# Keys through DRAM, one rounded maximum, and the low halves on VectorE in a fused attention and feed-forward block

## Chip, cores and metric

One NeuronCore of a Trainium2 chip runs the whole block in one launch. The metric is the device time in microseconds. Before the change the median of three runs is 3265.69 us (3263.84 to 3275.1).

## The reference

For 64 batches of 256 positions with 512 channels, and a context of the same shape:

```python
q, k, v = relu(heads(layernorm(x))), relu(heads(ctx)), relu(heads(ctx))   # 16 heads of 32
att = softmax(q @ k.T / sqrt(32))
x = x + tanh(g_xattn) * relu(concat(att @ v) @ ffn_w.T + ffn_b)
xn = layernorm(x); prev = xn shifted by one position (zero first)
r = sigmoid((mu_r * xn + (1 - mu_r) * prev) @ W_r.T)
k2 = (mu_k * xn + (1 - mu_k) * prev) @ W_k.T
x = x + tanh(g_ffn) * r * (square(relu(k2)) @ W_v.T)
```

## The kernel before

Products that need more than one rounded pass are made of two rounded halves, a high one (the value rounded to fp32r) and a low one (what the rounding left): high times high, low times high, high times low. Each tensor that enters such a product is thus split by two instructions: a rounding copy on ScalarE (`..._high`) and a difference (`..._low`). For the scores the three terms are stacked along the contraction: `q_st` and `k_st` hold, for each head, 96 rows of 32 channels (three combinations of halves), in four groups c of four heads.

The loop is software-pipelined by hand over the batches: `pipeline` (L203) runs `iteration(i, par)` on each engine, and each engine has its own written order. In one turn i, TensorE does the sixteen `shifted_scores(i, n)` with `scores` seven ahead (up to `scores(i + 1, 6)`), `values` and `denominators` of each group once the group's exponentials are there, and between them, in 32 pieces, the dense products of earlier batches: `key` (i - 2), `project` (i - 1), `receptance` and `value` (i - 2). Two banks of PSUM alternate for the scores, so `scores(n)` waits until `head_max(n - 2)` has read its bank; two more alternate for the shifted scores. One bank, `tp_bank`, serves all transposes (`turn_q`, `turn_m`, `turn_xn`) in turn. Engines wait only on semaphores; what stands behind a wait in an engine's order waits too.

Around the change, by engine:

- SyncE (L217): `load_k` (L242) loads the keys of group c three times, once for each 32-row block of `k_raw`; `load_x`; `move_m` (L251) moves the two halves of the negated maxima into rows 96 and 97 of `q_st`; `write_o` and `read_o` turn the attention's output through DRAM; `store`.
- GpSimd (L312): `rstd_1`, `rstd_2` (a power on one or two columns), and the low halves `k_low` (L335), `o_low` (L350), `xk_low`, `xr_low`, `ka_low`, the difference `x_diff` (L358) of neighbouring positions and the square `ka_square` (L384).
- ScalarE (L430): `k_high` (L480) writes relu(k), rounded, to all 96 rows of `k_st` and relu(k) in place in 32 rows of `k_raw`; the exponentials (L489); `q_stack` (L471) and `xt_copy` copy transposes out of `tp_bank`; `load_x1` and `load_v` issue transfers; other high halves.
- VectorE (L638): `head_max` (L688) reduces a bank of scores to `nmax`; `split_m` (L698) splits four heads' maxima into two halves, which `turn_m` then transposes and `copy_m` (L708) copies out; `norm_o` (L715) is a reciprocal of the denominators and a product, and waits for `denominators`; `add_x`, `norm_2`, `mix_k` (L750), `mix_r`, `stats_1` (L652), `finish` (L770), `relu_v` (L683), `q_low` (L675).
- TensorE (L857): `project(b, u)` (L965) starts with the bias product, then waits for `o_hi_ready` and `o_lo_ready`; `values` waits for `v_ready`.

VectorE's order in a turn begins with head_max 7 of batch i and ends with head_max 6 of batch i + 1; the other work stands between maxima, as in `head_max(i, 12)`, `copy_m(i, 2)`, `q_low(i + 1, 1)`, `norm_o(i, 0)`, `head_max(i, 13)`. TensorE's order there is `shifted_scores(i, 5)`, dense, `scores(i, 12)`, dense, `values(i, 0)`, `turn_m(i, 2)`, `denominators(i, 0)`, `shifted_scores(i, 6)`, `turn_q`, then the first piece of `project(i - 1, 1)`.

## Time and profile before

| | before |
|---|---|
| median of three runs | 3265.69 us |
| the profiled execution's own time | 3260.97 us |
| its span, first to last instruction | 3259.0 us |
| granted TensorE clock, mean | 0.987 |
| TensorE busy | 2905.3 us (89%) |
| VectorE busy | 2953.6 us (91%) |
| ScalarE busy | 2040.9 us (63%) |
| GpSimd busy | 1669.2 us (51%) |
| DMA | 308.95 MB, 95 GB/s, mean busy share of the 16 engines 31% |

A busy share is an average over the span. Which engine ends last at a given place is read in the timeline, from the idle time before an instruction and what released it. A matmul's end is modelled, so TensorE's busy time isn't its rate at its peak.

### The profile page before, as it was taken

To read this page: it belongs to the slowest core of one execution; us is meant where nothing else is said; L and a number is where in the kernel's file an instruction comes from. 1 tells how busy PE (TensorE), PEld (TensorE's weight loads), DVE (VectorE), ACT (ScalarE), POOL (GpSimd) and SP (SyncE) were. 2 spreads that over 40 slices of the span, in tenths; PEclk is the share of its full clock that TensorE was granted. 3 is DMA by queue.
4 is the path that set the end of the run, shared out by engine and by line. 5 is a ranking of instruction groups with operands and counts; after the bars stand their busy time and mean duration, and the time that the engine had idled before them with its cause. 6 is when DMAs were issued, how large, how long until landed. Compare 5 with 4: busy or idle time off the path is not lost. (4 is left out here: it accounts for less than half of the span.)

```text
span 3259.0 us, 74168 instructions
## 1 busy us (share of the span) xinstructions
PE 2905.3 (89%) x23168; PEld 2204.9 (68%) x23168; DVE 2953.6 (91%) x4559; ACT 2040.9 (63%) x3276; POOL 1669.2 (51%) x1158
## 2 busy tenths in 40 slices
PE   3899899999999999999899999999999999999998
PEld 2567666666667667667676666666666676666776
DVE  4899999999999999999999999999999999999984
ACT  4566666666666666666666666666666666666662
POOL 1455555555554554555555555545545545545553
PEclk9899999999999999999999999999999999999999
DMA  3333323323323323333233233233233233232331
GB/s 106 95 89 104 102 83 105 104 81 103 105 84 102 101 87 97 93 98 101 82 106 102 83 105 104 81 105 106 81 103 103 85 102 100 87 99 88 100 94 38
DMA packets 289548, 308.95 MB, mean 95 GB/s; under 512 B 162529, under 2 KB 197345, under 8 KB 289506
## 3 DMA queue, kind: packets, MB, share of 16 engines
q1 hardware_dynamic: 254690, 241.30, 25.0%
q10 hardware_dynamic: 34816, 67.12, 6.1%
q8 instruction: 24, 0.39, 0.0%
q14 instruction: 18, 0.15, 0.0%
HBM read 239.08 MB, written 67.11 MB: 94 GB/s over the span
## 5 line engine op out<-in xcount | busy, mean ns | idle before, releaser
L346 POOL TENSOR_TENSOR k_st<-k_raw,k_st 32x1024 fp32r<-32x1024 f32 x256 | 617.6, 2412 | 774.8 <-ACT k_raw L487 761.4
L694 DVE TENSOR_REDUCE nmax<-bank 128x2 f32<-128x512 f32 x1024 | 683.7, 684 | 64.3 <-PE bank L916 55.3
L498 ACT ACTIVATE probs<-bank 128x512 f32<-128x512 f32 x1024 | 595.2, 592 | 234.0 <-PE bank L928 229.7
L916 PE MATMUL bank<-k_st,q_st 96*128 96x256 f32 x2048 | 442.2, 298 | 79.1 <-DVE nmax L694 74.0
L916 PEld LDWEIGHTS bank<-k_st,q_st 96*128 96x128 f32 x2048 | 357.1, 193 | 160.4 <-DVE nmax L694 95.4
L723 DVE RECIPROCAL o_val<-bank 128x256 f32<-128x256 f32 x256 | 447.2, 1747 | 13.8 <-PE bank L954 9.9
L484 ACT ACTIVATE k_st<-k_raw 96x1024 fp32r<-96x1024 f32 x256 | 270.6, 1057 | 295.6 <-DMA k_raw<-ctx_t_dram 295.5
L928 PE MATMUL bank<-q_st,k_st 98*128 98x256 f32 x2048 | 441.4, 297 | 13.6 <-DMA q_st<-m_t 10.8
L928 PEld LDWEIGHTS bank<-q_st,k_st 98*128 98x128 f32 x2048 | 348.2, 192 | 85.4 <-issue 26.7
L476 ACT ACTIVATE q_st<-bank 96x512 fp32r<-96x512 f32 x512 | 303.0, 592 | 158.7 <-PE bank L884 157.1
L961 PE MATMUL bank<-xk_hi,w_hi 128*128 128x256 f32 x1024 | 299.0, 292 | 0.0
L942 PE MATMUL bank<-probs,v_pos 128*32 128x256 f32 x4096 | 278.1, 389 | 13.0 <-DVE v_pos L686 7.3
L961 PE MATMUL bank<-xk_lo,w_hi 128*128 128x256 f32 x1024 | 286.9, 280 | 0.0
L961 PE MATMUL bank<-xk_hi,w_lo 128*128 128x256 f32 x1024 | 286.8, 280 | 0.0
L954 PE MATMUL bank<-probs,ones_r 128*32 128x256 f32 x4096 | 280.7, 393 | 0.0
L487 ACT ACTIVATE k_raw<-k_raw 32x1024 f32<-32x1024 f32 x256 | 270.4, 1056 | 8.1
L884 PE MATMUL bank<-ident_r,q_nat 128*96 128x128 f32 x2048 | 220.7, 231 | 48.8 <-ACT q_st L476 31.3
L884 PEld LDWEIGHTS bank<-ident_r,q_nat 128*96 128x96 f32 x2048 | 191.4, 127 | 103.7 <-issue 73.5
L355 POOL TENSOR_TENSOR o_lo<-o_mv,o_hi 128x512 fp32r<-128x512 f32 x128 | 166.4, 1300 | 178.4 <-ACT o_hi L505 166.7
L388 POOL TENSOR_TENSOR xm<-xm 128x512 f32<-128x512 f32 x128 | 141.7, 1107 | 183.4 <-ACT xm L542 175.8
L757 DVE SCALAR_TENSOR_TENSOR xm<-xd,mu_sb,xt 128x256 f32<-128x256 f32 x256 | 229.9, 956 | 5.1 <-POOL xd L364 5.1
L332 POOL TENSOR_TENSOR rstd<-ve,mhalf 128x1 f32<-128x1 f32 x128 | 69.2, 541 | 300.0 <-DVE ve L741 185.6
(93 smaller groups left out, 7055.8 us busy)
## 6 DMA issues: line engine op xcount, KB each, us to landing
k_raw<-ctx_t_dram SPq DMA_DIRECT2D x768, 128.0 KB, 2.5
x_ln<-x_dram SPq DMA_DIRECT2D x256, 128.0 KB
v_pos<-ctx_dram ACTq DMA_DIRECT2D x64, 512.0 KB, 5.5
o_dram<-o_val SPq DMA_DIRECT2D x256, 128.0 KB, 1.7
o_mv<-o_dram SPq DMA_DIRECT2D x512, 64.0 KB, 2.1
x<-x_dram ACTq DMA_DIRECT2D x64, 512.0 KB, 3.3
out_dram<-x SPq DMA_DIRECT2D x64, 512.0 KB, 2.9
q_st<-m_t SPq DMA_DIRECT2D x512, 4.0 KB
```

The source lines that it names most:

```text
L346: nc.gpsimd.tensor_tensor(k_st[rows, c, :, :], k_raw[rows, :, :], k_st[rows, c, :, :].bitcast(F32), ALU.subtract).then_inc(k_lo_ready, 1)
L476: nc.scalar.activation(q_st[0:QK, c, :, P * u:P * u + P], tp_bank[0:QK, :].rearrange("p (g t) -> p g t", g=GR), ACT.Copy).then_inc(q_stack ...
L484: nc.scalar.activation(k_st[0:QK, c, :, :], k_raw[0:QK, :, :], ACT.Relu).then_inc(k_hi_ready, 1)
L498: nc.scalar.activation(probs[:, n // GR % 2, n % GR, :, :].rearrange("p v t -> p (v t)"), st_bank[n % 2][:, :], ACT.Exp, scale=SCALE).then ...
L694: nc.vector.tensor_reduce(nmax[:, :, n % GR:n % GR + 1], s_bank[n % 2][:, :].rearrange("p (u y) -> p u y", u=NU), AX_X, ALU.max, negate=Tr ...
L723: nc.vector.reciprocal(o_val[:, :], pv_bank[:, T:2 * T]).then_inc(rden_ready, 1)
L884: mm = nc.tensor.transpose(tp_bank[0:QK, P * g:P * g + P].bitcast(F32R), q_nat[:, u, GR * c + g, :, :], ident_r[:, :])
L916: mm = nc.tensor.matmul(s_bank[n % 2][:, T * u:T * u + T], q_st[0:QK, c, g, P * u:P * u + P], k_st[0:QK, c, g, :], start=True, stop=True)
L928: mm = nc.tensor.matmul(st_bank[n % 2][:, T * v:T * v + T], k_st[0:ST, c, g, P * v:P * v + P], q_st[0:ST, c, g, :], start=True, stop=True)
L942: nc.tensor.matmul(pv_bank[HD * g:HD * g + HD, 0:T], v_pos[:, v, HD * h:HD * h + HD], probs[:, c % 2, g, v, :], start=(v == 0), stop=(v == ...
L954: mm = nc.tensor.matmul(pv_bank[HD * g:HD * g + HD, T:2 * T], ones_r[:, 0:HD].bitcast(F32), moving, start=(n == 0), stop=(n == len(sums) - 1))
L961: mm = nc.tensor.matmul(dst, lhs[a], rhs[c], start=first and n == 0, stop=last and n == 2)
```

## The change

1. Keys. Each batch's keys are loaded once, 128 partitions by four groups (`load_k(b)`, four transfers). ScalarE rounds them in one instruction into a new tile `k_high` (`k_halve`), VectorE leaves the low half in `k_raw` (`k_low(b)`), both halves are written to a tensor `k_dram` in DRAM (`write_k`), and `stack_k` reads them back into the 96 rows of `k_st`, two transfers for each group. This begins two batches ahead, so the pipeline starts one iteration earlier. `k_high` of four groups on ScalarE and `k_low` of four groups on GpSimd go.
2. Maxima. They are written rounded by `head_max` itself, `split_m` goes, one row of `q_st` in place of two holds them, and `move_m` is one transfer.
3. `o_low`, `x_diff`, `xk_low`, `xr_low` and `ka_low` go from GpSimd to VectorE, `ka_square` to ScalarE. GpSimd keeps `rstd_1` and `rstd_2`.

```diff
@@ sync
-            def load_k(b, c):
-                    after(sp, k_hi_ready, CH * b + c)
-                    after(sp, k_lo_ready, CH * b + c)
-                    for r in range(3):
-                        sp.dma_start(k_raw[HD * r:HD * r + HD, :, :],
-                                     ctx_t[b][:, GR * c:GR * c + GR, :]).then_inc(k_loaded, 16)
+            def load_k(b):
+                    for g in range(GR):
+                        sp.dma_start(k_raw[g:P:GR, :, :],
+                                     ctx_t[b].rearrange("f (c g) t -> g f c t", g=GR)[g]).then_inc(k_loaded, 16)
+            def write_k(b, par):
+                    sp.wait_ge(k_hi_ready, b + 1)
+                    sp.wait_ge(k_lo_ready, b + 1)
+                    for half, tile in enumerate((k_high, k_raw)):
+                        sp.dma_start(k_dram[par, :, half].rearrange("c f g t -> (f g) c t"),
+                                     tile[:, :, :]).then_inc(k_written, 16)
+            def keys_written(b):
+                    sp.wait_ge(k_written, 32 * (b + 1))
+            def stack_k(b, c, par):
+                    after(sp, st_ready, HEADS * (b - 1) + GR * c + GR)
+                    sp.dma_start(k_st[0:2 * HD, c, :, :].bitcast(F32),
+                                 k_dram[par, c].rearrange("h f g t -> (h f) g t")).then_inc(k_stacked[c], 16)
+                    sp.dma_start(k_st[2 * HD:QK, c, :, :].bitcast(F32), k_dram[par, c, 0]).then_inc(k_stacked[c], 16)
             def iteration(i, par):
-                load_k(i, 3)
+                stack_k(i, 3, par)
                 store(i - 3, 1 - par)
                 move_m(i, 1)
                 write_o(i - 1, 3)
                 read_o(i - 1, 1)
-                load_k(i + 1, 0)
+                keys_written(i + 1)
+                load_k(i + 2)
+                stack_k(i + 1, 0, 1 - par)
                 move_m(i, 2)
                 write_o(i, 0)
-                load_k(i + 1, 1)
+                stack_k(i + 1, 1, 1 - par)
                 load_x(i + 2)
                 move_m(i, 3)
                 write_o(i, 1)
-                load_k(i + 1, 2)
+                stack_k(i + 1, 2, 1 - par)
                 move_m(i + 1, 0)
                 load_w(i)
                 read_o(i, 0)
                 write_o(i, 2)
+                write_k(i + 2, par)
@@ scalar
+            def k_halve(b):
+                    act.wait_ge(k_loaded, 16 * GR * (b + 1))
+                    after(act, k_written, 32 * b)
+                    nc.scalar.activation(k_high[:, :, :].bitcast(F32R), k_raw[:, :, :], ACT.Relu).then_inc(k_hi_ready, 1)
+            def ka_square(b, half):
+                    nc.scalar.activation(part, part, ACT.Square).then_inc(ka_ready, 1)
...
@@ vector
+            def k_low(b):
+                    dve.wait_ge(k_hi_ready, b + 1)
+                    nc.vector.scalar_tensor_tensor(out=k_raw[:, :, :].bitcast(F32R), in0=k_raw[:, :, :], scalar=0.0,
+                                                   in1=k_high[:, :, :], op0=ALU.max,
+                                                   op1=ALU.subtract).then_inc(k_lo_ready, 1)
             def iteration(i, par):
                 head_max(i, 7)
-                split_m(i, 1)
...
                 copy_m(i, 2)
                 q_low(i + 1, 1)
                 norm_o(i, 0)
+                o_low(i - 1, 1)
                 head_max(i, 13)
+                xr_low(i - 2)
...
                 norm_o(i, 1)
+                ka_low(i - 2, 0)
                 head_max(i + 1, 1)
+                ka_low(i - 2, 1)
+                x_diff(i - 1, 0)
                 head_max(i + 1, 2)
+                x_diff(i - 1, 1)
                 mix_k(i - 1)
                 head_max(i + 1, 3)
-                split_m(i + 1, 0)
                 copy_m(i + 1, 0)
                 head_max(i + 1, 4)
                 stats_1(i + 2)
                 finish(i - 2, 0, par)
+                xk_low(i - 1, 0)
                 head_max(i + 1, 5)
                 norm_o(i, 2)
+                xk_low(i - 1, 1)
                 head_max(i + 1, 6)
+                k_low(i + 2)
+                o_low(i, 0)
```

On ScalarE `ka_square` stands right behind each `kt_relu`, and `k_halve(i + 2)` behind `xt_copy(i - 1, 1)`. On TensorE `turn_m` waits for `head_max`'s own count, and `scores` of a group's first head wait for `k_stacked[c]`.

## Rows read from the trace of the kernel before

**Rows 1.** The page's first part: busy time of each engine.

```profile
span 3259.0 us, 74168 instructions
PE 2905.3 (89%) x23168; PEld 2204.9 (68%) x23168; DVE 2953.6 (91%) x4559; ACT 2040.9 (63%) x3276; POOL 1669.2 (51%) x1158
```

**Rows 2.** Timeline, TensorE: start, duration (us), engine, line, tiles, shape, count, idle before.

```profile
1506.45 1.07 PE L954 MATMUL bank<-probs,ones_r 128*32 128x256 f32 x16
...
1516.60 0.28 PE L893 MATMUL bank<-ident_r,m_nat 128*8 128x128 f32 x2 [1.11 <-DVE m_nat L705]
...
1527.58 0.28 PE L893 MATMUL bank<-ident_r,m_nat 128*8 128x128 f32 x2 [0.70 <-DVE m_nat L705]
...
1540.38 1.07 PE L942 MATMUL bank<-probs,v_pos 128*32 128x256 f32 x16
...
1541.59 1.07 PE L954 MATMUL bank<-probs,ones_r 128*32 128x256 f32 x16
...
1543.50 0.40 PE L961 MATMUL bank<-w_hi,o_hi 128*128 128x512 f32 x1
...
1552.65 0.65 PE L902 MATMUL bank<-ident_r,xn 128*128 128x128 f32 x4 [1.04 <-DVE xn L747]
...
1555.27 1.07 PE L954 MATMUL bank<-probs,ones_r 128*32 128x256 f32 x16
```

**Rows 3.** Timeline, VectorE, between the second and third mark.

```profile
1519.66 1.99 DVE L666 TENSOR_SCALAR ve<-mv 128x2 f32<-128x2 f32 x1
1521.56 0.68 DVE L774 SCALAR_TENSOR_TENSOR th<-th,bank 128x512 f32<-128x512 f32 x1
1522.27 0.75 DVE L777 SCALAR_TENSOR_TENSOR x<-th,tgh,x 128x512 f32<-128x512 f32 x1
1522.94 0.68 DVE L694 TENSOR_REDUCE nmax<-bank 128x2 f32<-128x512 f32 x1
1523.54 1.75 DVE L723 RECIPROCAL o_val<-bank 128x256 f32<-128x256 f32 x1
...
1525.66 1.28 DVE L694 TENSOR_REDUCE nmax<-bank 128x2 f32<-128x512 f32 x2
```

**Rows 4.** Timeline, VectorE, the same instruction as at 1519.66, 20 turns later.

```profile
2506.97 2.09 DVE L666 TENSOR_SCALAR ve<-mv 128x2 f32<-128x2 f32 x1
```

**Rows 5.** Timelines of ScalarE's queue and of VectorE around V.

```profile
1533.99 0.42 ACTq L460 DMA_DIRECT2D v_pos<-ctx_dram  x1
...
1539.43 0.69 DVE L686 TENSOR_SCALAR v_pos<-v_pos 128x1024 f32<-128x1024 f32 x1 [0.31 <-DMA v_pos<-ctx_dram]
```

**Rows 6.** Timeline, GpSimd, two of its `k_low` instructions.

```profile
1511.01 2.39 POOL L346 TENSOR_TENSOR k_st<-k_raw,k_st 32x1024 fp32r<-32x1024 f32 x1 [0.22 <-POOL xd L364]
...
1519.25 2.37 POOL L346 TENSOR_TENSOR k_st<-k_raw,k_st 32x1024 fp32r<-32x1024 f32 x1 [1.61 <-ACT k_raw L487]
```

**Rows 7.** Timeline, VectorE, between the first and second mark, and one `mix_r`.

```profile
1511.24 3.63 DVE L757 SCALAR_TENSOR_TENSOR xm<-xd,mu_sb,xt 128x256 f32<-128x256 f32 x4
1514.80 0.68 DVE L694 TENSOR_REDUCE nmax<-bank 128x2 f32<-128x512 f32 x1
1515.51 0.76 DVE L703 CAST m_nat<-nmax 128x8 fp32r<-128x8 f32 x1
...
1531.32 1.66 DVE L766 SCALAR_TENSOR_TENSOR xd<-xd,mu_sb,xt 128x256 f32<-128x256 f32 x4
```

**Rows 8.** Groups by line and form: count, busy us, mean ns, idle before.

```profile
L732 DVE SCALAR_TENSOR_TENSOR x<-xn,tg,x 128x512 f32<-128x512 f32 x128 | 204.6, 1598 | 8.8 <-ACT xn L513 8.8
...
L649 DVE TENSOR_TENSOR w_lo<-x,w_hi 128x1024 fp32r<-128x1024 f32 x2 | 2.4, 1215 | 0.0
...
L432 ACT ACT_TABLE_LOAD x1 | 1.3, 1283 | 0.8 <-PEq L1193 0.8
```

**Rows 9.** V's landings, then the page's DMA issues (count, KB, us to landing).

```profile
DMA to landing us min/median/max: 3.2/5.5/6.4
...
out_dram<-x SPq DMA_DIRECT2D x64, 512.0 KB, 2.9
```

More of the change, by code:

```diff
@@ L44, in flamingo_block @@
     QK = 3 * HD
[L45 removed]
+    ST = QK + 1
     es = ExitStack()
@@ L138, in flamingo_block @@
         v_ready = sem("v_ready")
-        k_pos = sem("k_pos")
+        k_written = sem("k_written")
+        k_stacked = [sem(f"k_stacked{c}") for c in range(CH)]
         k_hi_ready = sem("k_hi_ready")
@@ L203, in pipeline @@
         def pipeline(eng, iteration):
-            for i in range(-1, 4):
+            for i in range(-2, 4):
                 iteration(i, i % 2)
@@ L255, in move_m @@
                     sp.wait_ge(m_copied, CH * b + c + 1)
-                    for piece in range(2):
-                        sp.dma_start(q_st[QK + piece:QK + piece + 1, c, :, :].bitcast(F32),
-                                     m_t[GR * piece:GR * piece + GR, :].bitcast(F32)).then_inc(m_moved[c % 2], 16)
+                    sp.dma_start(q_st[QK:QK + 1, c, :, :].bitcast(F32),
+                                 m_t[0:GR, :].bitcast(F32)).then_inc(m_moved[c % 2], 16)
             def write_o(b, c):
@@ L333, in rstd_2 @@
                                             ALU.pow).then_inc(rstd2_ready, 1)
-            def k_low(b, c, *before):
-                if on(b):
-                    for batch, s, count in before:
-                        if on(batch):
-                            after(pool, s, count)
-                    pool.wait_ge(k_pos, CH * b + c + 1)
-                    pool.wait_ge(k_hi_ready, CH * b + c + 1)
-                    rows = slice(2 * HD, 3 * HD)
-                    nc.gpsimd.tensor_tensor(k_st[rows, c, :, :], k_raw[rows, :, :], k_st[rows, c, :, :].bitcast(F32),
-                                            ALU.subtract).then_inc(k_lo_ready, 1)
-                    pool.wait_ge(k_lo_ready, CH * b + c + 1)
@@ L411, in iteration @@
                 rstd_2(i - 1, 0)
                 rstd_2(i - 1, 1)
-                x_diff(i - 1, 0)
-                ka_low(i - 2, 0)
-                ka_low(i - 2, 1)
-                x_diff(i - 1, 1)
-                k_low(i + 1, 1,
-                      (i - 1, xd_ready, 2 * (i - 1) + 2), (i - 2, ka_lo_ready, 2 * (i - 2) + 2),
-                      (i - 1, rstd2_ready, 2 * (i - 1) + 2))
-                xk_low(i - 1, 0)
-                xk_low(i - 1, 1)
-                k_low(i + 1, 2,
-                      (i - 1, xk_lo_ready, 2 * (i - 1) + 2))
@@ L424, in iteration @@
-                o_low(i, 0)
             pipeline(pool, iteration)
@@ L614, in iteration @@
                 xt_copy(i - 1, 1)
-                k_high(i + 1, 1)
+                k_halve(i + 2)
                 exponent(i, 11)
@@ L768, in mix_r, with o_low, x_diff, xk_low @@
                     last.then_inc(xr_ready, 1)
+            def o_low(b, u):
+                if on(b):
+                    dve.wait_ge(o_hi_ready, NU * b + u + 1)
+                    after(dve, z_ready, NU * (b - 1) + u + 1)
+                    nc.vector.tensor_tensor(by_tile(o_lo, u), o_mv[:, :, :].rearrange("p g (k a) -> p k g a", k=KC),
+                                            by_tile(o_hi, u).bitcast(F32), ALU.subtract).then_inc(o_lo_ready, 1)
+            def x_diff(b, u):
+                if on(b):
+                    dve.wait_ge(xt_ready, NU * b + u + 1)
+                    after(dve, xr_hi_ready, b)
+                    after(dve, xr_lo_ready, b)
+                    nc.vector.tensor_tensor(xd[:, :, P * u:P * u + P], xt[:, :, 1 + P * u:1 + P * u + P],
+                                            xt[:, :, P * u:P * u + P], ALU.subtract).then_inc(xd_ready, 1)
+            def xk_low(b, half):
+                if on(b):
+                    dve.wait_ge(xk_ready, 2 * b + half + 1)
+                    dve.wait_ge(xk_hi_ready, 2 * b + half + 1)
+                    after(dve, kt_ready, 2 * b)
+                    part = slice(2 * half, 2 * half + 2)
+                    nc.vector.tensor_tensor(xk_lo[:, part, :], xm[:, part, :], xk_hi[:, part, :].bitcast(F32),
+                                            ALU.subtract).then_inc(xk_lo_ready, 1)
+            def xr_low(b):
+                if on(b):
+                    dve.wait_ge(xr_ready, b + 1)
+                    dve.wait_ge(xr_hi_ready, b + 1)
+                    after(dve, r_ready, NU * b)
+                    nc.vector.tensor_tensor(xr_lo[:, :, :], xd[:, :, :], xr_hi[:, :, :].bitcast(F32),
+                                            ALU.subtract).then_inc(xr_lo_ready, 1)
+            def ka_low(b, half):
+                if on(b):
+                    dve.wait_ge(ka_ready, 2 * b + half + 1)
+                    dve.wait_ge(ka_hi_ready, 2 * b + half + 1)
+                    after(dve, vv_ready, NU * b)
+                    nc.vector.tensor_tensor(ka_lo[:, 2 * half:2 * half + 2, :], xm[:, 2 * half:2 * half + 2, :],
+                                            ka_hi[:, 2 * half:2 * half + 2, :].bitcast(F32),
+                                            ALU.subtract).then_inc(ka_lo_ready, 1)
             def finish(b, u, par):
@@ L801, in iteration @@
                 relu_v(i)
-                split_m(i, 2)
                 split_low(i, 3)
```

114 lines of the change are left out of this document (25 added, 89 removed).

## The prediction

> **What bounds the kernel now.** I read the page's busy shares first: TensorE 89%, VectorE 91%, ScalarE 63%, GpSimd 51% of 3259.0 us [rows 1]. Two engines are close to full and neither is full, so the next view is the timeline of one turn of the steady loop (one batch), once for TensorE and once for VectorE. I place everything on four marks of TensorE that recur each turn, in the program's names: D1 (`denominators(i, 1)`, 1506.45), TM0 (`turn_m(i + 1, 0)`, 1516.60), TM1 (`turn_m(i, 1)` of the next turn, 1527.58), D0 (`denominators(i, 0)`, 1541.59), and D1 again at 1555.27 [rows 2]. The four stretches are 10.15, 10.98, 14.01 and 13.68 us, a turn of 48.82. This turn is on the short side: `stats_1`'s last instruction recurs from 1519.66 to 2506.97 over 20 turns, 49.37 each [rows 3, 4].
>
> Who ends last differs by stretch. In D1 to TM0 and TM0 to TM1 VectorE runs without a break and TensorE waits at the end for the maxima. In TM1 to D0 TensorE waits for VectorE and for V: `values(i, 0)` starts at 1540.38 [rows 2], just after `relu_v`, which itself waited 0.31 us for the transfer of V [rows 5]. In D0 to D1 the wait is at `turn_xn`, 1.04 us for VectorE [rows 2].
>
> Why VectorE is so full is in the durations. The tiny `ve` instruction of L666, 128x2, took 1.99 us from 1519.66; GpSimd's `k_low` ran 1519.25 to 1521.62 [rows 3, 6]. The four L757 instructions took 3.63 us from 1511.24, and GpSimd's `k_low` ran 1511.01 to 1513.40; four of the same shape in L766 took 1.66 [rows 6, 7]. VectorE instructions with SBUF operands stand still until GpSimd's instruction ends. The Trainium skill (SBUF — State Buffer, section Who interferes with whom) says this is an exclusive lock, held for the whole instruction, for which a VectorE instruction with two SBUF inputs or in a two-port mode competes; this trace agrees, 1.99 us against about 0.17 for what the instruction needs. By that page alone the move off GpSimd would be worth all that VectorE now loses; it is rival 1 below.
>
> **The change, stretch by stretch.** Durations: a difference of two 128x1024 tensors on VectorE took 1.22 us [rows 8], `finish`'s two 128x512 forms 0.68 and 0.75 [rows 3]. Consecutive instructions overlap a little: 128x512 steps start 0.60 after one another (1522.94 to 1523.54 for `head_max`), `norm_o` is 2.12 in all (1523.54 to 1525.66), `finish` 1.38 (1521.56 to 1522.94) [rows 3]. I take 0.61 for each moved 128x512 difference, 1.15 for the two of 1024 columns (`xr_low`, `k_low`); the far end, if they don't overlap at all, is 0.69 and 1.22. The sum per turn: eight of 0.61 and two of 1.15, 7.2 us more on VectorE. Against it `split_m` goes (four times CAST and difference) and so do the locks; GpSimd keeps three tiny powers.
>
> D1 to TM0. VectorE now: waits, norm_o 2.12, two head_max, L757 from 1511.24, head_max at 1514.80, then `split_m`, whose CAST alone took 0.76 from 1515.51 behind GpSimd [rows 7]. After: L757 falls from 3.56 to 1.58 (-1.98), `split_m` from the maximum's end 1515.48 to TM0 at 1516.60 becomes a bare handover of 0.1 (-1.02), and VectorE, at norm_o 0.28 sooner since its queue ahead is shorter (-0.28). Added: ka_low twice and x_diff twice, 2.44, plus 0.13 since `mix_k` must wait for the x_diff right before it to finish. 10.15 - 3.28 + 2.57 = 9.45 us (9.8 at the far end).
>
> TM0 to TM1. VectorE is busy throughout [rows 3]. Removed: 1.8 of L666, and `split_m` 0.5. Added: xk_low twice, o_low(i, 0) (1.83), k_low 1.15, and 0.15 for `finish` behind GpSimd's `rstd_1`: 3.1 us. 10.98 - 2.3 + 3.1 = 11.8 (12.1). Queued behind k_low and o_low stand head_max 7, on which `turn_m` and `scores` 9 wait. TensorE alone would need about 10.2 here, so this stretch gets longer by 0.8.
>
> TM1 to D0. VectorE's locks here (norm_1) go and ScalarE loses `k_high`, so TensorE alone would be at `values(i, 0)` some 11.6 us after TM1 (12.8 less the two waits that TensorE has there, 1.2 us together). But V comes too late: `load_v` is issued 6.4 us after TM1 (1533.99), behind q_stack of the third-slot transposes, which I move to 6.0; it lands 5.4 us later here and 5.5 in the median of 64 [rows 5, 9]; `relu_v` takes 0.7. That puts `values` at 12.3 instead of 12.8. Then 1.2 to D0. 13.5 us, between 12.8 (V in time) and 14.0 (as now).
>
> D0 to D1. The wait of 1.04 at `turn_xn` goes: add_x and norm_2 no longer stand behind GpSimd, and VectorE has over 1 us to spare there. But a new wait comes. `project(i - 1, 1)` needs o_lo, which GpSimd had ready long before; after the change VectorE makes it behind `norm_o(i, 0)`, and norm_o waits for D0 itself. From D0: 1.07 for the group and 0.15 for the handover, 2.12 for norm_o, 0.67 for o_low and 0.05 back, 4.1 us. TensorE reaches the first product that needs it 1.9 us after D0 (1543.50) [rows 2]. It stands 2.2 us, and starts again 0.1 slower. 13.68 - 1.04 + 2.3 = 14.9 us. Nothing covers this: all of TensorE's later work is queued behind.
>
> Sum: 9.45 + 11.8 + 13.5 + 14.9 = 49.65 us for a turn without disturbance. The turn before, with the median of its own V wait, is 49.1, and 49.4 with the disturbed turns in it (some of them 2 to 3 us longer); I leave that share in. So +0.55 us a turn, over 62 full turns +34 us.
>
> **Edits that I cost at nothing.** ScalarE: eight activations on keys go, one of that size and two squares come; it stood at 63%, and its handovers to TensorE lie after other waits. SyncE's queue: a batch's keys were twelve loads of 128 KB; now four loads, two writes of 512 KB and eight reads from DRAM come, 3 MB instead of 1.5. A stack's reader is at least 7 us away, so they are covered; without the cover a read costs up to the 2.9 us of a larger store [rows 9]. One of the two moves of m goes, covered by the two slots of TensorE work ahead. The keys pass through `write_k`, on which SyncE waits for `k_low`; behind it stand stack_k(3), store and move_m(i, 1). k_low ends before copy_m(1) can, so move_m isn't held by the wait, only by bytes in the queue (rival 3). Start: the first keys make a round trip to DRAM before the first scores, about +4 us; the end is a chain through x_diff, xk_low, xr_low and ka_low, which get shorter, about -4 us.
>
> The profiled execution took 3260.97, so 3295 on its scale; the median of the runs shown is 4.7 above it, and the forecast is 3300 us.
>
> **Rivals.**
> 1. The lock is all that matters: VectorE's load of 46 us a batch (2953.6 over 64 [rows 1]) gains 7.2, loses `split_m` (four times 0.5 at least) and the locks: 1.8 and 2.0 above, 1.7 in L732 (a mean of 1598 ns, twice a turn, where L777 took 0.75 for the same shape [rows 3, 8]), and as much again in other lines by my estimate. At 42 to 44 us the loop becomes TensorE's. TensorE's own work in a turn is 44 to 45 us (91% busy inside the loop), with the o_low wait 46.5. Then 49.4 becomes 46.5 to 48.7, 3085 to 3220 us. For it: the locks are plain in the rows. Against it: in each of the two VectorE stretches the additions were laid against the removals one by one, and they nearly cancel.
> 2. V arrives in time and nothing else changes: TM1 to D0 at 12.8, a turn of 48.95 and with disturbances 49.2, 3252 us, no change. For it: the shortest landing of the 64 was 3.2 us [rows 9]. Against: o_mv and the new k loads share the engines at that moment.
> 3. The slower side by another mechanism, the queue of SyncE: write_k's 1 MB, stack_k's 384 KB and the 512 KB of the store are issued just ahead of move_m(i, 1). A 512 KB store takes 2.9 us to land [rows 9]; the bytes need 6 us or so, and m is copied 3 us after k_low. `shifted_scores(i, 4)` wants it 7.4 us after TM1, I find it landed at 6.2. It decides once m lands over 1.2 us later than that; every us beyond is 62 us, so 3360 and up.
> 4. `Square` isn't in the loaded activation tables. The one load now seen takes 1.28 us [rows 8]; four a turn (two squares, each between exponentials) are 5 us of ScalarE, and push exponentials late by up to 2.6: 3380. I hold it unlikely, since Relu, Copy, Exp and Tanh already share one load. The Trainium skill (ScalarE: Activation LUTs, Table sets) gives about 2.7 us for each switch, drain included; by it the same case would be double, and no row here shows a switch.
>
> **How the numbers follow.** Main case 0.55: 3300, by its own bounds 3240 to 3355 (V as above -0.5 a turn, overlap of the new instructions +0.65); four fifths of it is slower by over 0.5%, one fifth within. Rival 1 0.20, faster. Rival 2 0.13, mostly no change. Rival 3 0.09 and rival 4 0.03, slower. 0.5% (16 us) is about what a measurement of this kernel can tell from no change. Faster 0.23, same 0.22, slower 0.55. The range 3225 to 3360 leaves out most of rival 1 and rival 3's upper part.
>
> **What would show it.** In the profile after: no VectorE instruction stretched beyond its shortest form (`ve` at 0.17 us); VectorE near 87% busy and GpSimd under 4%; TensorE waiting about 2.2 us a turn for VectorE's o_lo in the second half of `project`; `turn_m` of the first and second groups still waiting for `head_max`; `values` waiting for relu_v and that for V; no wait of the shifted scores on m. The prediction is wrong if the wait for o_lo is missing, if TM0 to TM1 comes out under 11 us, or if new table loads or waits on q_st appear.

## The result and the profile after

The changed kernel takes 3435.58 us in the median (3425.87 to 3445.88), the kernel before 3265.34 beside it: a ratio of 1.0515, interval 1.0476 to 1.0554. It is slower, as forecast, but by 170 us where I had forecast 34, and above the range that I gave. First the page of the kernel after, its busy shares and the granted clock of TensorE in 40 slices; they answer to [rows 1].

```profile
span 3437.6 us, 70851 instructions
...
PE 2978.9 (87%) x23168; PEld 2248.3 (65%) x23168; DVE 2697.7 (78%) x4687; ACT 1643.7 (48%) x2956; POOL 115.6 (3%) x198
...
PEclk9899999999999999999999999999999999999999
```

VectorE did 256 us less than before although it has 128 instructions more, and yet the span grew by 179. TensorE's idle time grew by 105 us and its busy time by 74, for the same 23168 matmuls. So most of the 179 us went into waits, and the rest into longer products, for which the clock further down accounts in part. The four marks of one turn (TensorE's timeline, kernel after) answer to [rows 2]. L877 is `turn_m`, L925 `values`, L937 `denominators`, L944 a dense product.

```profile
1594.39 1.07 PE L937 MATMUL bank<-probs,ones_r 128*32 128x256 f32 x16
...
1603.94 0.28 PE L877 MATMUL bank<-ident_r,m_nat 128*4 128x128 f32 x2 [0.95 <-DVE m_nat L640]
...
1615.45 0.28 PE L877 MATMUL bank<-ident_r,m_nat 128*4 128x128 f32 x2 [0.74 <-DVE m_nat L640]
...
1629.35 1.07 PE L925 MATMUL bank<-probs,v_pos 128*32 128x256 f32 x16 [0.75 <-issue]
...
1630.56 1.07 PE L937 MATMUL bank<-probs,ones_r 128*32 128x256 f32 x16
...
1646.89 1.07 PE L937 MATMUL bank<-probs,ones_r 128*32 128x256 f32 x16
```

D1, TM0, TM1, D0 and D1 again stand at 1594.39, 1603.94, 1615.45, 1630.56 and 1646.89, a turn of 52.50. Over all turns, from the starts of the same marks (each stretch is the sum of the medians of its parts):

| stretch | before | forecast | after |
|---|---|---|---|
| D1 to TM0 | 10.2 | 9.45 | 9.55 |
| TM0 to TM1 | 10.9 | 11.8 | 11.5 |
| TM1 to D0 | 14.4 | 13.5 | 15.5 |
| D0 to D1 | 13.6 | 14.9 | 16.4 |
| whole turn, mean of 61 | 49.41 | 49.95 | 52.40 |

(The forecast turn is 49.65, and 0.3 for disturbed turns.) The stretches that VectorE ends came out as worked out. The other two hold the whole miss, 2.0 and 1.5 us. (In the means of the same turns D0 to D1 is 15.9, since in some turns it is short; the miss there is then 1.0.) The view by who waited for what (kernel after: engine, line, releaser, us in all, times, longest) has two rows to which none of the kernel before answers.

```profile
ACT probs L431 <- DMA out_dram<-x: 190.4, 60, 5.0
...
PE bank L944 <- DVE o_lo L711: 136.9, 64, 3.0
```

The second is the forecast wait for `o_low`, 2.1 us a turn. The first, 3.2 us a turn of ScalarE, was not foreseen. It is an exponential that waits for the store of the output, which has nothing to do with it. The queues show why: first SyncE's (L256 `write_k`, L268 and L270 `stack_k`, L299 `store`, L277 `move_m`), then ScalarE's, both around TM1 at 1615.45.

```profile
1614.19 0.39 SPq L256 DMA_DIRECT2D k_dram<-k_high  x1
1614.62 0.51 SPq L256 DMA_DIRECT2D k_dram<-k_raw  x1
1615.66 0.58 SPq L268 DMA_DIRECT2D k_st<-k_dram  x1
1616.29 1.32 SPq L270 DMA_DIRECT2D k_st<-k_dram  x1
1617.91 0.39 SPq L299 DMA_DIRECT2D out_dram<-x  x1
1618.44 0.63 SPq L277 DMA_DIRECT2D q_st<-m_t  x1
```

```profile
1618.96 0.60 ACT L412 ACTIVATE q_st<-bank 96x512 fp32r<-96x512 f32 x1 [4.61 <-PE bank L868]
1622.16 0.38 ACTq L390 DMA_DIRECT2D x<-x_dram  x1
1622.66 0.60 ACT L431 ACTIVATE probs<-bank 128x512 f32<-128x512 f32 x1 [3.11 <-DMA out_dram<-x]
...
1624.07 0.38 ACTq L396 DMA_DIRECT2D v_pos<-ctx_dram  x1
```

L390 is `load_x1(i - 1)`. It loads into the buffer that the store empties, so it waits for the store's landing, and it is issued from ScalarE's own order: the exponential and the load of V stand behind it. Before, the store was issued 1.4 us after TM1 and landed in 2.9, and `load_x1` went out 4.5 after TM1 (medians of the turns). Now the store is issued 2.4 after TM1, behind 1 MB of `write_k` and the reads of `stack_k`, lands in 4.1 (median of 64, up to 6.3), and `load_x1` goes out 6.6 after TM1.

The wait itself isn't new. In the kernel before, SyncE's and ScalarE's timelines show the same order (L279 `store`, L487 the end of `k_high(i, 3)`, L454 `load_x1`):

```profile
1529.14 0.44 SPq L279 DMA_DIRECT2D out_dram<-x  x1
```

```profile
1531.61 1.05 ACT L487 ACTIVATE k_raw<-k_raw 32x1024 f32<-32x1024 f32 x1
1532.16 0.38 ACTq L454 DMA_DIRECT2D x<-x_dram  x1
```

This store landed at 1532.01 and `load_x1` went out at 1532.16, so there too the landing decided; in the median of the turns it went out 0.1 us behind the landing. But ScalarE was busy with `k_high` until 1532.66, and the wait cost nothing. The change takes that cover away and makes the landing later as well.

The chain of waits of the turn shown of the kernel after (start, us, what) passes through all of it:

```profile
1612.90 1.23 DVE k_raw L624
...
1614.62 0.51 SPq L256
1615.66 0.58 SPq L268
1616.29 1.32 SPq L270
1617.91 4.10 DMA out_dram<-x
...
1622.66 0.61 ACT probs L431
1623.31 0.52 PE bank L911 x2
```

The piece shown starts at VectorE's `k_low`. V is on this path too: it goes out 8.5 us after TM1 and lands in 5.0, and with `relu_v` (0.7) and the handover behind it that is where `values` starts, 14.3 after TM1 (medians). The store of an old batch is on the path that sets the end, 7% of the whole span by the page's chain.

The last stretch, D0 to D1, shows a thing beside the wait (TensorE's timeline, kernel after, behind D0):

```profile
1632.15 0.47 PE L953 MATMUL bank<-b_rows,ones_r 128*128 128x512 f32 x1
1634.76 0.76 PE L944 MATMUL bank<-w_hi,o_hi 128*128 128x512 f32 x1 [2.13 <-DVE o_lo L711]
1635.32 0.63 PE L944 MATMUL bank<-w_hi,o_lo 128*128 128x512 f32 x1
1635.74 0.63 PE L944 MATMUL bank<-w_lo,o_hi 128*128 128x512 f32 x1
...
1637.84 0.39 PE L944 MATMUL bank<-w_lo,o_hi 128*128 128x512 f32 x1
1638.07 0.40 PE L944 MATMUL bank<-w_hi,o_hi 128*128 128x512 f32 x1
```

The products behind the wait start 0.42 apart and take 0.63 us, those from 1637.84 on 0.23 apart and 0.40. The windows of the kernel after (us, busy and count of each engine, granted clock, DMA share, GB/s) say what that is:

```profile
1616.00:1626.00 10.00, 9.62 (x81) 8.13 (x73) 7.51 (x14) 3.91 (x8) 0.00 (x0) 1.00 0.81 256
1626.00:1634.00 8.00, 5.41 (x51) 3.30 (x51) 5.73 (x9) 6.56 (x12) 0.00 (x0) 1.00 0.64 186
1634.00:1638.00 4.00, 3.24 (x10) 2.83 (x11) 1.77 (x4) 0.60 (x1) 0.00 (x0) 0.57 0.10 33
1638.00:1648.00 10.00, 10.00 (x82) 7.15 (x81) 7.39 (x17) 5.37 (x10) 1.08 (x2) 1.00 0.29 92
```

TensorE had been at 1.00 of 2.4 GHz, busy for 9.62 of 10 us and then, with the waits for exponentials, V and o_lo, for 5.41 of 8. It stood still for 2.13 us and came back at the lower level, 1.2 GHz, for some 3 us. D0 to V1 (`values(i, 1)`, of the second group) is 12.7 us in the median and 11.3 at its tenth percentile; it is over 12 in 35 of 61 turns. So the lower clock costs about 1.4 us in over half of the turns, on top of the wait.

### The profile page after: what moved, and what is told of

It reads as the page before. It is cut to its first block, busy times and chain, and to the rows that moved or that the text cites. A ratio compares the mean times of both kernels' runs of the same rounds, so it can differ in the third digit from the quotient of the medians.

```text
span 3437.6 us, 70851 instructions
## 1 busy us (share of the span) xinstructions
PE 2978.9 (87%) x23168; PEld 2248.3 (65%) x23168; DVE 2697.7 (78%) x4687; ACT 1643.7 (48%) x2956; POOL 115.6 (3%) x198
## 4 chain that ended last, share of the span: by engine, by line
PE 34%; DVE 31%; issue 13%; DMA 8%; SPq 6%; ACT 4%; ACTq 2%; DVEq 1%; POOL 0%; POOLq 0%
PE bank L944 18%; DVE o_val L659 10%; DMA out_dram<-x 7%; DVE m_nat L640 6%; PE bank L925 4%; PE bank L911 4%; PE bank L899 3%; DVE xm L693 2%; SPq L270 2%; DVE st L594 2%; PE bank L937 2%; DVE k_raw L624 2%; ACT probs L431 2%; SPq L256 2%; SPq L268 2%
## 5 line engine op out<-in xcount | busy, mean ns | idle before, releaser
L640 DVE TENSOR_REDUCE m_nat<-bank 128x2 fp32r<-128x512 f32 x1024 | 696.1, 685 | 172.6 <-PE bank L899 170.8
L911 PE MATMUL bank<-q_st,k_st 97*128 97x256 f32 x2048 | 455.5, 304 | 71.6 <-ACT probs L431 53.8
L911 PEld LDWEIGHTS bank<-q_st,k_st 97*128 97x128 f32 x2048 | 346.4, 194 | 170.8 <-ACT probs L431 73.7
L944 PE MATMUL bank<-w_hi,o_hi 128*128 128x512 f32 x512 | 233.0, 455 | 136.9 <-DVE o_lo L711 136.9
L925 PE MATMUL bank<-probs,v_pos 128*32 128x256 f32 x4096 | 277.2, 388 | 75.2 <-issue 66.9
L944 PE MATMUL bank<-xk_hi,w_hi 128*128 128x256 f32 x1024 | 302.9, 296 | 26.1 <-DVE xk_lo L729 26.1
L944 PE MATMUL bank<-xk_lo,w_hi 128*128 128x256 f32 x1024 | 286.4, 280 | 0.0
L944 PE MATMUL bank<-xk_hi,w_lo 128*128 128x256 f32 x1024 | 285.9, 279 | 0.0
L937 PE MATMUL bank<-probs,ones_r 128*32 128x256 f32 x4096 | 277.0, 388 | 0.0
L649 DVE CAST m_t<-bank 4x256 fp32r<-4x256 f32 x256 | 105.1, 410 | 177.9 <-PE bank L877 177.8
L925 PEld LDWEIGHTS bank<-probs,v_pos 128*32 128x32 f32 x4096 | 112.5, 109 | 196.8 <-issue 139.4
L944 PEld LDWEIGHTS bank<-xk_hi,w_hi 128*128 128x128 f32 x1024 | 192.7, 188 | 62.7 <-issue 62.6
L944 PE MATMUL bank<-w_hi,o_lo 128*128 128x512 f32 x512 | 221.7, 433 | 0.0
L944 PE MATMUL bank<-w_lo,o_hi 128*128 128x512 f32 x512 | 219.1, 428 | 0.0
L944 PEld LDWEIGHTS bank<-w_hi,o_hi 128*128 128x128 f32 x512 | 108.1, 211 | 160.5 <-issue 151.9
```

The lines of the kernel that those rows point to most:

```text
L640: nc.vector.tensor_reduce(m_nat[:, c % 2, :, n % GR:n % GR + 1], s_bank[n % 2][:, :].rearrange("p (u y) -> p u y", u=NU), AX_X, ALU.max, n ...
L649: nc.vector.tensor_copy(m_t[0:GR, :], tp_bank[0:GR, 0:T]).then_inc(m_copied, 1)
L911: mm = nc.tensor.matmul(st_bank[n % 2][:, T * v:T * v + T], k_st[0:ST, c, g, P * v:P * v + P], q_st[0:ST, c, g, :], start=True, stop=True)
L925: nc.tensor.matmul(pv_bank[HD * g:HD * g + HD, 0:T], v_pos[:, v, HD * h:HD * h + HD], probs[:, c % 2, g, v, :], start=(v == 0), stop=(v == ...
L937: mm = nc.tensor.matmul(pv_bank[HD * g:HD * g + HD, T:2 * T], ones_r[:, 0:HD].bitcast(F32), moving, start=(n == 0), stop=(n == len(sums) - 1))
L944: mm = nc.tensor.matmul(dst, lhs[a], rhs[c], start=first and n == 0, stop=last and n == 2)
```

## The experiments

Two things were to be told apart: what the ScalarE wait costs, what the `o_low` wait with its clock costs, and then which part of the change pays and which loses. A figure in us is the median; a ratio is to the kernel before, run beside it, with its interval. That kernel took 3277.3 (e1 to e4), 3278.8 (e5, e6, b1, b2) and 3288.3 us (e7 to e10) there and 3265.3 beside the changed one, so gains over the changed kernel, given here as differences of medians, come out 12 to 23 us larger by ratios.

**e1: `load_x1` two exponentials later.** The x load is taken out from ahead of the exponential and of V's load.

```diff
-                load_x1(i - 1, 1 - par)
...
                 exponent(i, 3)
+                load_x1(i - 1, 1 - par)
```

> The changed kernel with one line moved on ScalarE: load_x1(i - 1), which waits for the store of batch i - 3 to land, is issued behind exponent(i, 3) in place of ahead of exponent(i, 2). Theory A (ScalarE stands behind the late store, 3.2 us a turn, and passes it on to TensorE through the exponentials and through V): the wait of the exponentials on out_dram goes from 190 us to near nothing, the stretch from TM1 to D0 falls from 15.5 to 13.5 us, and the time from 3436 to about 3310 us. Theory B (that wait is hidden, and the stretch is long because V and the key traffic are late whatever ScalarE does): under 30 us gained, 3400 or more.

Measured 3240.4, ratio 0.9889 (0.9859 to 0.9918): 195 us less than the changed kernel, more than expected of the wait alone. The wait for the store is gone, and V lands 3.6 us after its issue where it took 5.0. Both rows are of e1, by who waited:

```profile
PE bank L944 <- DVE o_lo L711: 135.4, 64, 2.4
...
ACT probs L431 <- DMA out_dram<-x: 0.9, 1, 0.9
```

From D3 (`denominators(i - 1, 3)`, just after TM1) to `values`, 14.11 became 11.23 with no spread (11.23 to 11.24 from the tenth to the ninetieth percentile), the length of TensorE's own work. So the late store, with V behind it, cost 2.9 us a turn, some 180 us, and it was the whole of that stretch's miss and more. Most of this is what ScalarE did late, V's issue above all: had V gone out at 6.0 and landed in 5.0, `values` could have started some 0.3 us later than it does in e1 (my estimate from the durations above). The wait for o_lo is untouched, but only 27 of 61 turns still have the long D0 to V1, where 35 had it; that is most of the rest of the 195 us.

**e2: `o_low(i - 1, 1)` two places earlier, ahead of `copy_m(i, 2)`.**

```diff
+                o_low(i - 1, 1)
                 copy_m(i, 2)
                 q_low(i + 1, 1)
                 norm_o(i, 0)
-                o_low(i - 1, 1)
```

> The changed kernel with one line moved on VectorE: o_low(i - 1, 1) ahead of copy_m(i, 2) in place of behind norm_o(i, 0). Theory A (TensorE's wait of 2.1 us a turn for o_lo, and the half clock that follows it in about two turns of three, 1.4 us each time): D0 to D1 falls from 16.3 us to 13.0, the granted clock rises from 0.974 to at least 0.985, the time to about 3230 us. Theory B (the wait only moves to the next handover, since VectorE's sum of work sets the turn): D0 to D1 shorter but TM0 to TM1 or D1 to TM0 longer by as much, under 60 us gained, 3375 or more.

Measured 3230.0, ratio 0.9856 (0.9827 to 0.9885): 206 us less, as expected. The wait for o_lo is gone. D0 to V1 is 8.91 us where it was 12.73, the granted clock of the whole run 0.995 instead of 0.974, and the wait for the store still 190.5 us. The step of 0.68 us had stood behind norm_o's 2.12 and its wait for D0, and its place alone cost the 206 us.

**e4: eight dummy products in the wait.** This leaves the wait for o_lo alone and keeps TensorE busy in it: the bias product is done eight times more, each result overwritten by the next.

```diff
+                        for _ in range(8 if u == 1 else 0):
+                            nc.tensor.matmul(dense_bank[u][:, :], ones_r[:, :], b_rows[:, :], start=True, stop=True)
                         nc.tensor.matmul(dense_bank[u][:, :], ones_r[:, :], b_rows[:, :], start=True, stop=False)
```

> The changed kernel with eight more copies of the bias product (their results are overwritten by the one that counts) on TensorE, ahead of its wait for o_lo in project(i - 1, 1): 1.9 us of matmuls into the gap of 2.1 us, the wait itself stays. Theory A (TensorE standing still there is what the clock answers with its lower level): the half-clock stretches behind that gap go, the granted clock rises to about 0.985 or more, D0 to V1 comes to 11.3 us in all turns, and the time falls by 1.0 us a turn, to about 3375 us. Theory B (the clock falls for another reason, the gap costs only itself): no change, 3436 us, or slower by what the copies overhang.

Measured 3375.4, ratio 1.0305 (1.0274 to 1.0337): 60 us less than the changed kernel, with 512 products more. TensorE's timeline of e4:

```profile
1642.42 2.09 PE L954 MATMUL bank<-b_rows,ones_r 128*128 128x512 f32 x8
1644.34 0.40 PE L955 MATMUL bank<-b_rows,ones_r 128*128 128x512 f32 x1
1645.00 0.47 PE L944 MATMUL bank<-w_hi,o_hi 128*128 128x512 f32 x1 [0.26 <-DVE o_lo L711]
1645.31 0.40 PE L944 MATMUL bank<-w_hi,o_lo 128*128 128x512 f32 x1
```

The first product that needs o_lo comes as late as before, but the clock holds: 0.40 us each, D0 to V1 is 11.29 to 11.33 from the tenth to the ninetieth percentile, none of 61 is over 12, granted clock 0.995. So the lower clock had cost 60 us, and the standing still the rest of e2's 206, some 145.

**e3: both edits, e1 and e2.**

> Both moves of the two runs before, in one kernel. If the two causes are independent, their gains add: 3436 less 125 and 205 gives about 3105 us, under the kernel before. If both are paid out of the same slack, or VectorE becomes the bound once both are gone, the gain is that of the larger one alone, 3200 us or more.

Measured 3162.8, ratio 0.9666 (0.963 to 0.9702): faster than before by 3.3%, but 58 us over the figure expected. Alone the edits bring 195 and 206 us, together 273. The rows of e3 that are new:

```profile
DVE o_lo L711 <- ACT o_hi L438: 172.1, 63, 4.2
ACT o_hi L438 <- DMA o_mv<-o_dram: 166.5, 64, 3.8
```

With `values` at its earliest, the attention's output (`o_mv`) has not come back through DRAM yet: its last read lands 13.7 us after TM1 in the median, and D0 is at 12.65. `o_low` has no slack any more at its earlier place, and D0 to V1 is 10.43 instead of 8.91. `copy_m` stands behind it on VectorE, and TensorE waits for that, 74 us in 51 turns. 13 turns are over 12 us again, and the clock is 0.988. In e1 the same wait for o_mv is 172.0 us and hides. Little slack was there to begin with: in the kernel before, o_mv landed 12.4 us after TM1, and GpSimd's `o_low` began 1.1 us before D0 and took 1.3.

**e5 and e6: the whole of SyncE's order changed.** The store and `move_m` come first, `stack_k(i, 3)` and `write_k` behind `read_o`, and what waits for `write_k` behind that: in e5 on the changed kernel, in e6 on e3.

```diff
             def iteration(i, par):
-                stack_k(i, 3, par)
                 store(i - 3, 1 - par)
                 move_m(i, 1)
                 write_o(i - 1, 3)
                 read_o(i - 1, 1)
+                stack_k(i, 3, par)
+                write_k(i + 1, 1 - par)
+                move_m(i, 2)
...
```

> The changed kernel with SyncE's order alone changed: store, move_m(i, 1), write_o(i - 1, 3) and read_o(i - 1, 1) go out first, then stack_k(i, 3) and the 1 MB of write_k, then move_m(i, 2), keys_written, stack_k(i + 1, 0) and load_k. ScalarE's order is as in the changed kernel, load_x1 ahead of exponent 2. Theory A (the store lands late only because write_k's and stack_k's bytes are ahead of it in the queue): ScalarE's wait on out_dram goes as in the run with load_x1 moved, and the time comes to about 3240 us again; the wait for o_lo and the half clock behind it stay. Theory B (the store is late because finish is): ScalarE still waits over 2 us a turn and the time stays above 3380.

> The kernel with both moves, and SyncE's order of the run before too. In the kernel with both moves VectorE waits 2.7 us a turn for o_high, which waits 2.6 us for o_mv, whose write and read stand behind the same bytes. Theory A: with the bytes behind them, o_mv lands in time, D0 to V1 comes to 8.9 us in place of 10.4, no half clock is left in the loop, a turn is 46.4 us and the time about 3065 us. Theory B (o_mv is late by write_o's own wait for norm_o, not by the queue): the wait on o_mv stays over 1.5 us a turn and the time above 3120.

Both missed: e5 3593.6, ratio 1.0978 (1.0942 to 1.1014), and e6 3450.5, ratio 1.0533 (1.0501 to 1.0565), 158 and 288 us worse than what they were built on. In e5 the wait for the store did fall, to 52.3 us, but the scores of the fourth group now wait for their keys:

```profile
PE bank L899 <- DMA k_st<-k_dram: 204.7, 59, 4.8
```

`stack_k(i, 3)` had no slack to give: behind `read_o`, which waits for o, its reads went out 7.4 to 7.6 us after TM1, where they had gone out within 0.2 of it. In e6 the same wait is 246.1 us. TensorE's stand-stills there are followed by the lower clock as well: in e5 it is at 1.2 GHz for 179 us of the stretch TM1 to D0, in the changed kernel for 5, and the granted clock of the profiled runs is 0.947 and 0.952. Two steps were moved at once, and e5 and e6 can't tell what `write_k` alone is worth.

**e10: `write_k` and what waits for it behind `read_o`, `stack_k(i, 3)` kept first.** On the changed kernel. **e7: the same with e1 and e2.**

```diff
                 stack_k(i, 3, par)
                 store(i - 3, 1 - par)
                 move_m(i, 1)
                 write_o(i - 1, 3)
                 read_o(i - 1, 1)
+                write_k(i + 1, 1 - par)
+                move_m(i, 2)
...
                 write_o(i, 2)
-                write_k(i + 2, par)
```

> The changed kernel with write_k and what waits for it later in SyncE's order, and stack_k(i, 3) left where it is, first in the turn (in the run with SyncE's order alone changed it had been moved behind read_o, and scores 12 waited 3.2 us a turn for it). Theory A (the store is late by the 1 MB ahead of it): ScalarE's wait on out_dram falls under 1 us a turn, no new wait on k_st, TM1 to D0 falls from 15.5 us to about 13, and with the o_lo wait and the half clock left, about 3260 us. Theory B (bytes are late anywhere in the turn, since the queue as a whole is too full): the wait moves to another transfer, over 3380.

> That order of SyncE together with the two moves (load_x1 behind exponent 3, o_low(i - 1, 1) ahead of copy_m(i, 2)). In the kernel with both moves alone VectorE waited 2.7 us a turn for o_high and that for o_mv. Theory A (write_k's bytes delay o_mv): the wait on o_mv falls under 1 us, D0 to V1 comes to 8.9 us, no half clock in the loop, a turn is 46.4 us, about 3065 us. Theory B (o_mv is late by its own chain): no faster than 3163.

e10 measured 3382.5, ratio 1.0284 (1.023 to 1.0339): only 53 us less (76 by ratios), far from the lower of the figures expected and at the upper one. The store is issued 1.0 us earlier and lands in 2.9 us again (median; 4.1 in the changed kernel). So what `write_k` had put ahead of it made it late: its wait for `k_low`, its own bytes, or the reads of `stack_k` that it had held back, which now go out 3 us sooner; e10 doesn't tell these apart. The exponential waits 53.4 us in place of 190.4. These 53.4 are what the loss of `k_high` lays bare, with the store as early as in the kernel before; b2 below, which keeps `k_high` there, has 2.0 us of this wait in all. The other 137 come from the queue. But `load_x1` still goes out just ahead of V's load, and now the writes go out beside both. VectorE's wait for V in the changed kernel, and then in e10:

```profile
DVE v_pos L631 <- DMA v_pos<-ctx_dram: 107.5, 61, 2.8
```

```profile
DVE v_pos L631 <- DMA v_pos<-ctx_dram: 163.6, 62, 3.3
...
ACT probs L431 <- DMA out_dram<-x: 53.4, 60, 2.6
```

V goes out 6.3 us after TM1 in place of 8.5 but lands 6.1 us after its issue (5.0 before the edit), and D3 to `values` is 13.08, 1.0 us better. Half of that is lost again in D0 to D1, whose mean rises from 15.9 to 16.4: 50 of 61 turns now have the long D0 to V1. Why the same wait for o_lo brings the lower clock in more turns here was not tested. The delay in TM1 to D0 was two things in a row, a wait that kept ScalarE from issuing V and a crowd of transfers that kept V from landing, and e10 trades much of the one for the other. e1 removes both because x's load leaves V's place altogether.

e7 measured 3084.4, ratio 0.9393 (0.9348 to 0.9437): 78 us better than e3, 19 over the figure expected. `write_o` lands in 1.7 us where it took 3.1, and `read_o` goes out 5.5 us after TM1 in place of 6.8, so the o_mv wait of e3 fell from 166.5 to 97.8 us; that is 1.6 a turn, where under 1 was expected. The clock is 0.995.

**b1: of the whole change only the rounded maxima.** On the kernel before: `head_max` writes `m_nat`, one row of q_st holds them, `split_m` goes; keys and low halves stay as they were.

```diff
-                    nc.vector.tensor_reduce(nmax[:, :, n % GR:n % GR + 1],
+                    nc.vector.tensor_reduce(m_nat[:, c % 2, :, n % GR:n % GR + 1],
...
-                split_m(i, 1)
```

> The kernel before with only the part on the maxima: head_max writes them rounded, split_m goes, one row of q_st, one transfer in move_m. GpSimd keeps all it had. Theory A (split_m stood on the handover from the maxima to turn_m): each of D1 to TM0 and TM0 to TM1 gets shorter by 0.5 to 1.0 us, 60 to 110 us faster than before, about 3190. Theory B (the locks by GpSimd take up what VectorE gains): within 0.5% of before.

Measured 3159.3, ratio 0.9635 (0.9603 to 0.9667), more than expected. The turn is 47.84 in the mean where it was 49.41. I had priced `split_m` at 1.0 and 0.5 in the two stretches that VectorE ends. They gave 0.9 and 0.3, D0 to D1 gave another 0.2, so the sum fits and its places only in part. The granted clock is 0.993 where it was 0.987.

**b2: the whole change, but the keys as before.** `k_high` stays on ScalarE and `k_low` of four groups on GpSimd; all other low halves and differences are on VectorE, the squares on ScalarE.

> The whole change except the keys: maxima rounded, low halves and differences on VectorE, squares on ScalarE, in the changed kernel's order; keys are loaded three times and split by k_high on ScalarE and k_low on GpSimd, four times a batch, as before. The low half on GpSimd is a 32x1024 difference of 2.4 us, so four locks a turn stay. Theory A (the route through DRAM costs 2.9 us a turn by ScalarE's wait for the store, and frees VectorE of the locks, 2 to 3 us where they fall on the stretches that VectorE bounds): both nearly cancel, 3340 to 3440 us. Theory B (the route through DRAM is the loss and the locks of k_low fall where VectorE has room): about 3240 us.

Measured 3591.6, ratio 1.0962 (1.0932 to 1.0992); every figure expected was too low. Groups by line of b2 (count, busy, mean ns, idle before):

```profile
L728 DVE TENSOR_TENSOR xr_lo<-xd,xr_hi 128x1024 fp32r<-128x1024 f32 x64 | 145.9, 2279 | 5.1 <-issue 4.8 <-ACT xr_hi L463 0.3
...
L602 DVE TENSOR_SCALAR ve<-mv 128x2 f32<-128x2 f32 x64 | 114.0, 1782 | 2.2
```

As long as `k_low` runs on GpSimd, VectorE has the added work and its standing still: `xr_low` takes 2279 ns, in the changed kernel 1215. From b1 to b2 the moves onto VectorE cost 432 us. By stretch (means of 61 turns) that is 2.3 us in D1 to TM0, 2.0 in TM0 to TM1, nothing in TM1 to D0, and 2.6 in D0 to D1, where the wait for o_lo is. From b2 to the changed kernel the keys through DRAM give 156 back (146 by ratios): the stretches that VectorE ends get shorter by 2.0 and 1.2 as its standing still goes, TM1 to D0 longer by 1.1 by the queue. In b2 TensorE is also at 1.2 GHz for 193 us of TM0 to TM1, in the changed kernel for 5; what this costs there was not separated. The parts of the change, added in this order, are thus about -119, +432 and -156; another order was not measured.

**e8 and e9: two more steps on e7.** e8 puts `k_low(i + 1)` behind `head_max(i, 9)`, away from the two maxima that `turn_m` waits for; e9 also moves `o_low(., 0)`.

```diff
                 head_max(i, 9)
+                k_low(i + 1)
...
                 head_max(i + 1, 6)
-                k_low(i + 2)
```

> The kernel of the run before with VectorE's k_low moved out of the stretch from TM0 to TM1, which VectorE bounds, into the stretch after it (behind head_max 9, one turn later). Theory A (in that stretch VectorE's sum of work is the time): TM0 to TM1 falls from 11.5 to about 10.4 us, 65 to 70 us faster than the run before. Theory B (the wait moves to the next handover): under 20 us.

> The kernel of the run before with o_low(i, 0) too moved out of that stretch, behind copy_m(i, 1) of the next turn. By the same sum another 0.6 us a turn, 38 us, until TensorE bounds the stretch at about 10.2 us, so 15 to 38 us. If TensorE is the bound already: nothing.

e8 measured 3030.2, ratio 0.923 (0.9185 to 0.9275), 54 us under e7, a little less than expected: `turn_m`'s wait for the maxima at TM1 is gone (from `values(i - 1, 3)` to TM1 it is 1.00 us in place of 1.81). e9 measured 3028.7, ratio 0.9216 (0.9171 to 0.926), no gain that can be told from none. The page of e8 shows what bounds it:

```profile
PE 2863.1 (95%) x23168; PEld 2193.1 (72%) x23168; DVE 2679.3 (88%) x4687; ACT 1657.4 (55%) x2956; POOL 114.8 (4%) x198
```

TensorE is at 95% of 3027.4 us, in turns of 45.90 us. This is the version to keep: the changed kernel's instructions with the places of a few steps changed, 7.7% faster than the kernel before, 11.8% faster than the changed one.

## Why the prediction was right or wrong

**D1 to TM0, right.** 9.45 forecast, 9.55 measured. **TM0 to TM1, right.** 11.8 forecast, 11.5 measured. In both TensorE waits at the end for the maxima, as worked out. The durations that carried it hold. Groups by line, kernel after; `ve` is the instruction of [rows 3] that took 1.99:

```profile
L729 DVE TENSOR_TENSOR xk_lo<-xm,xk_hi 128x512 fp32r<-128x512 f32 x128 | 87.3, 683 | 0.0
...
L624 DVE SCALAR_TENSOR_TENSOR k_raw<-k_raw,k_high 128x1024 fp32r<-128x1024 f32 x64 | 77.7, 1214 | 0.0
...
L604 DVE TENSOR_SCALAR ve<-mv 128x2 f32<-128x2 f32 x64 | 10.8, 169 | 2.2
```

With GpSimd's large steps gone no VectorE step is stretched, and b2 shows the stretching back with only `k_low` on GpSimd. That much of rival 1 is shown.

**TM1 to D0, the step that failed.** Forecast 13.5, measured 15.5. The term that failed is V's issue, put at 6.0 us after TM1: it went out at 8.5 (6.0 in the median of the kernel before, too). Among the edits costed at nothing I wrote that ScalarE's "handovers to TensorE lie after other waits", and of the queue I asked only who reads the stacks and m. Rival 3 had the right queue and the right bytes, but the wrong reader: the shifted scores waited on m four times in the whole run, 17.7 us. (Once the other waits are gone it shows: 47.7 us in e7, 53.2 in e8.) The reader that decided was `load_x1`, which waits for the store, and which holds everything that ScalarE does behind it. In taking `k_high` off ScalarE I also took away the work that had hidden this wait, and counted it only as a gain. e1 gives the term its price: 2.9 us a turn against the changed kernel, some 180 us of its 195. That `values` waits for V's transfer was right; that this comes at 12.3 can't be seen by itself, since V went out late.

**D0 to D1, the wait right, its price too low.** I foresaw the wait for o_lo, its cause and its length (2.2 us forecast, 2.13 and 2.1 in the mean measured), and put the restart at 0.1. (Nor had GpSimd had o_lo ready "long before" in the kernel before: it was there some 0.2 us after D0, 1.7 ahead of its use.) The restart was at the lower clock in over half of the turns, 1.4 us each; e4 measures that as 60 us, over a third of the miss. e2 shows that the whole of it, 206 us, hung on the place of one step in VectorE's order. The forecast gain of 1.04 at `turn_xn` came (2.10 to 1.00 in the medians).

**The waits together.** In means of the 61 turns the two terms are 2.1 and 1.0 us over the forecast, less 0.3 in TM0 to TM1 and plus 0.1 in D1 to TM0. The whole turn is 52.40 against 49.95, 2.45 over, with 0.3 for disturbed turns already in the forecast; times 62 that is 152 us, and the miss in the median is 136. The profiled spans differ by 179 us, and 62 times the 2.99 that the mean turn grew is 185, so start and end hold next to nothing of it.

**Slower, as forecast, but in part by luck.** e1 lacks only the wait that I had not foreseen, and it is 1.1% faster than the kernel before. With TM1 to D0 at the 13.5 that I forecast in place of e1's 12.65 it would stand near 3293 (my estimate, 62 times 0.85 more), no clear change. So the sign came from the stretch whose mechanism I had wrong.

**VectorE's load, too high.** I forecast near 87%, it is 78%. Part of that is only the longer span. In work, 87% of 3300 is 44.9 us a batch, and 2697.7 over 64 is 42.2. The instructions that both kernels have, form by form, took 9.0 us a batch less (sum of their durations). My rows had shown 5.5 of it, and the rest I had put into rival 1, whose 42 to 44 holds the figure. The surplus lay where VectorE had slack before and moved no stretch.

**The rivals.** Rival 1, TensorE alone sets the time, 3085 to 3220: it didn't come in the changed kernel. With the two waits out of the way e7 comes to 3084, although VectorE still ends TM0 to TM1 there; e8, where TensorE is 95% busy, is the case itself, at 3030 and so below the range. What stood against it was less VectorE's load than the order of a few steps. Rival 2 (V in time, 3252) is e1 in that stretch: 12.65 from TM1 to D0 against its 12.8. Rival 4, a table for `Square`, is out: the trace has one table load, of 1283 ns, as before.

## What to carry to other kernels

A transfer that an engine issues with a wait in front stands in that engine's own order: before bytes are added to a queue, list who waits for each later landing in that queue, and what computes behind those waits, not only who reads the data. A step moved to a full engine is placed by its reader, one place ahead of whatever waits for something itself; here `o_low` ahead of `norm_o` rather than behind it was worth 206 us. A wait on TensorE in a loop that is otherwise full is priced with its restart at both levels of the clock.

## What the runs showed of the hardware

- A stand-still of 2.13 us, after 10 us in which TensorE was 96% busy and 8 in which it was 68% busy, all at 2.4 GHz, was followed by about 3 us at 1.2 GHz (granted clock 0.57 from 1634 to 1638), and so in 35 of 61 turns. A wait for o_lo of about 2 us did it in 27 of 61 in e1 and 50 in e10. Eight products that serve no purpose in the gap took the granted clock of the run from 0.974 to 0.995 and 60 us from its time.
- A 512 KB store that goes out behind 1 MB of writes and 384 KB of reads lands in 4.1 us in the median, and in 2.9 with the writes behind it and the reads 3 us further ahead (e10). V's load lands in 3.6 us with the x load behind it (e1), in 5.0 with it ahead (changed kernel; 5.5 in the kernel before), and in 6.1 with the 1 MB of writes following besides (e10).
- VectorE's instructions were stretched beside GpSimd's: `ve` took 1.93 us in the mean with `k_low` and the rest on GpSimd, 1.78 with `k_low` alone there (b2), and 0.17 with neither; `xr_low` 2.28 in b2 and 1.22 without.
- Moves onto VectorE that I had priced at 6.03 us a turn (eight of 0.61 and `xr_low`'s 1.15), 374 us in all and more than nothing only where VectorE ends a stretch, cost 432 while `k_low` still ran on GpSimd. Stretched instructions, the wait for o_lo (137.3 us) and a granted clock of 0.950 (0.993 in b1) are all in that; how it splits among them was not measured.
